# Attention scores of two heads at once in 64-row tiles, in the middle stage of a gated cross-attention block

## The reference, cut to what matters

```python
def _L1_xattn_ref(x, latents, mask, g1, b1, g2, b2, Wq, Wkv, Wout):
    heads, dim_head = (16, 64)
    xn = layer_norm(x, g1, b1)              # x: the context, 16 x 375 x 256
    ln_lat = layer_norm(latents, g2, b2)    # latents: 16 x 112 x 256
    q = ln_lat @ Wq
    kv = jnp.concatenate([xn, ln_lat], axis=1) @ Wkv      # 487 tokens
    k, v = jnp.split(kv, 2, axis=-1)
    ...
    weight = jnp.einsum('bhld,bhnd->bhln', q * scale, k * scale)   # 112 x 487 per head
    weight = jnp.where(full_mask[:, None, None, :], weight, neg)
    weight = jax.nn.softmax(weight.astype(jnp.float32), axis=-1)
    out = jnp.einsum('bhln,bhnd->bhld', weight, v)
    return out.transpose(0, 2, 1, 3).reshape(b, l, heads * dim_head) @ Wout
```

## Time and profile before

| | |
|---|---|
| time, median of 3 runs | 1531.09 us (1529.65 to 1533.0) |
| the profiled execution | 1528.29 us, of which the traced span is 1526.3 us |
| TensorE busy | 1357.1 us, 89% of the span |
| VectorE busy | 1177.2 us, 77% |
| ScalarE busy | 954.2 us, 63% |
| GpSimd busy | 654.9 us, 43% |
| middle stage, first scores to the end of the last batch's slots | 525.0 to 1290.0 us of the span |

### The profile page before, as it was taken

One profiled execution on the slowest core, in us unless ns is written; L12 is line 12 of the kernel. 1 busy time (PEld: TensorE's weight loads), 2 busy tenths in 40 slices (PEclk: granted clock), 3 DMA queues, 4 the chain that ended last, 5 costly groups with the idle time before them and its releaser, 6 DMA issues. The chain is left out here.

```text
span 1526.3 us, 45153 instructions
## 1 busy us (share of the span) xinstructions
PE 1357.1 (89%) x14276; PEld 1053.6 (69%) x14276; DVE 1177.2 (77%) x3350; ACT 954.2 (63%) x2456; POOL 654.9 (43%) x1044
## 2 busy tenths in 40 slices
PE   5999999999974799999999999999999997279995
PEld 3788888888751367776776677767766776278994
DVE  4899999999863388887887877878878787267772
ACT  4887888888951366665666665656656666045663
POOL 3544444444543234342543344334534424235654
PEclk8999999999976899999999999999999999589998
DMA  5333333333201666346653565447634671473323
GB/s 163 100 117 115 115 101 115 115 111 97 72 8 34 130 135 127 88 90 129 144 110 69 120 144 108 91 94 145 125 80 96 130 160 48 136 287 55 61 40 73
DMA packets 167807, 163.36 MB, mean 107 GB/s; under 512 B 81274, under 2 KB 155394, under 8 KB 164528
## 3 DMA queue, kind: packets, MB, share of 16 engines
q1 hardware_dynamic: 151440, 118.80, 34.2%
q0 software_dynamic: 13168, 35.80, 9.3%
q10 hardware_dynamic: 3024, 6.47, 1.5%
HBM read 64.48 MB, written 41.96 MB: 70 GB/s over the span
## 5 line engine op out<-in xcount | busy, mean ns | idle before, releaser
L1414 PE MATMUL b_ps_p<-b_tok_s,w_s 128*128 128x112 f16 (+1 forms) x1536 | 223.3, 300 | 11.3 <-DVE b_k_s L1698 6.6
L1709 DVE CUSTOM_DVE_ANT_0 b_prob<-b_ps_s,b_keep 112x487 f32<-112x487 f32 x256 | 167.9, 656 | 27.4 <-PE b_ps_s L1493 26.3
L1414 PE MATMUL b_ps_p<-w_s,b_tok_s 128*122 128x512 f16 x768 | 186.9, 379 | 0.0
L1605 ACT ACTIVATE b_prob<-b_prob,b_top 112x487 f32<-112x487 f32 x256 | 177.6, 694 | 10.5 <-DVE b_top L1709 10.3
L1414 PEld LDWEIGHTS b_ps_p<-b_tok_s,w_s 128*128 128x128 f16 x1536 | 117.5, 100 | 95.9 <-issue 17.9
L1611 ACT ACTIVATE b_pT<-b_ps_t 122x448 f16<-122x448 f32 x256 | 137.7, 538 | 72.1 <-PE b_ps_t L1501 69.6
L1493 PE MATMUL b_ps_s<-b_k_stack,b_q_dup 128*112 128x487 f16 x512 | 153.4, 382 | 25.6 <-issue 15.9
L1714 DVE TENSOR_TENSOR b_pT<-b_ps_t,b_pT 122x448 f16<-122x448 f32 x256 | 158.6, 619 | 6.9 <-ACT b_pT L1611 5.5
L701 ACT ACTIVATE a_prob<-a_prob,a_top 112x375 f32<-112x375 f32 x256 | 156.4, 611 | 4.4 <-DVE a_top L837 3.4
L837 DVE CUSTOM_DVE_ANT_0 a_prob<-a_ps_s,a_keep 112x375 f32<-112x375 f32 x256 | 138.2, 540 | 24.4 <-PE a_ps_s L593 21.8
L1521 PEld LDWEIGHTS b_ps_o<-b_v_s,b_pT 122*128 122x128 f16 x3072 | 122.5, 98 | 44.3 <-issue 6.6
(11 more groups left out here) (259 smaller groups left out, 3062.1 us busy)
## 6 DMA issues: line engine op xcount, KB each, us to landing
b_k_stack<-b_k_s SPq DMA_DIRECT2D x64, 487.0 KB, 11.0
xs<-a_blank SPq DMA_DIRECT2D x14, 1032.0 KB, 4.0
b_q_dup<-b_q_s SPq DMA_DIRECT2D x128, 112.0 KB, 5.2
c_w_pool<-w_split SPq DMA_DIRECT2D x8, 1600.0 KB, 10.5
b_wch_f<-in_w_experts POOLq DMA_DIRECT2D x32, 384.0 KB, 11.8
w_split<-b_wch_s POOLq DMA_DIRECT2D x32, 384.0 KB, 7.2
a_ctx_f<-in_ctxT SPq DMA_DIRECT2D x16, 375.0 KB, 3.7
a_k_stack<-a_k_s SPq DMA_DIRECT2D x64, 93.8 KB, 2.8
```

What stands on the lines that cost most here:

```text
L1414: last = pe.matmul(out, sta(a, k), mov(m, k), start=(k == 0 and n == 0), stop=(k == tiles - 1 and n == 2))
L1605: act.activation(prob[:, h % RING, 0:NK], prob[:, h % RING, 0:NK], ACT.Exp, bias=top[:, h % RING:h % RING + 1], scale=-1.0, accum_out=sums ...
L1709: dve.tensor_tensor_reduce(prob[:, h % RING, 0:NK], ps_s[h % 2][0:T, 0:NK], keep[par][:, :], -SCALE1, 3e38, ALU.add, ALU.min, top[:, h % R ...
```

## The change

`scores` is called once for two heads, in even slots. It reads the keys and the queries as the products leave them, from `k_s` and `q_s`, which are now double: head `2j` lies in rows 0 to 63 and head `2j+1` in rows 64 to 127. For each of the three `PASSES` it issues two matmuls of 64 rows, one into each score bank, so a pair of heads has six matmuls of 64 rows where it had four of 128 rows. The product of the two low parts is no longer computed. One semaphore increment covers both heads; before a pair TensorE waits for the maxima of both heads before it (`s_max` up to `2 * pair`), where head `h` waited for head `h-2` alone. `k_stack`, `q_dup`, SyncE's `stack` with its 12 transfers for each batch, and the two semaphores go away. The built program gives these matmuls a tile of 64 rows by 128 columns at row 0 or row 64 of the array; every other matmul, before and after, has a tile of 128 rows.

```diff
@@ -1025,10 +1025,8 @@
         keep = [sb(f"keep{i}", [T, NK], F32) for i in range(2)]
 
 
-        q_s = sb("q_s", [128, 2, IT, T], F16)
-        q_dup = [sb(f"q_dup{i}", [128, 2, H, T], F16) for i in range(2)]
-        k_s = sb("k_s", [128, 2, IT, NK], F16)
-        k_stack = [sb(f"k_stack{i}", [128, H, NK], F16) for i in range(2)]
+        q_s = [sb(f"q_s{i}", [128, 2, IT, T], F16) for i in range(2)]
+        k_s = [sb(f"k_s{i}", [128, 2, IT, NK], F16) for i in range(2)]
         v_s = [sb(f"v_s{i}", [128, 2, NB1, INNER], F16) for i in range(2)]
 
 
@@ -1104,8 +1102,6 @@
         s_item = sem("item")
         s_ihi = sem("ihi")
         s_ifree = sem("ifree")
-        s_kstack = sem("kstack")
-        s_qdup = sem("qdup")
         s_score = sem("score")
         s_max = sem("max")
         s_exp = sem("exp")
@@ -1182,22 +1178,6 @@
                 need(sp, s_keep, 1, c, 0, settled)
                 sp.dma_start(keep_u[:, :], mask[c].partition_broadcast(T)).then_inc(s_mload, 16)
 
-            def stack(c, par):
-
-
-                need_all(sp, settled, (s_ihi, PI, c, P_Q), (s_ifree, PI, c, P_Q), (s_score, H, c - 1, 1))
-                for a in range(2):
-                    for part in (HI, LO):
-                        src = k_s[64 * a:64 * a + 64, part, :, :]
-                        rows = part if a == 0 else 1 - part
-                        sp.dma_start(k_stack[par][64 * rows:64 * rows + 64, a::2, :], src).then_inc(s_kstack, 16)
-                need_all(sp, settled, (s_ihi, PI, c, P_V), (s_ifree, PI, c, P_V))
-                for a in range(2):
-                    for rows in range(2):
-                        for part in (HI, LO):
-                            sp.dma_start(q_dup[par][64 * rows:64 * rows + 64, part, a::2, :],
-                                         q_s[64 * a:64 * a + 64, part, :, :]).then_inc(s_qdup, 16)
-
             def residual(c):
                 need(sp, s_hfree, HI_, c, 0, settled)
                 sp.dma_start(x_res[:, :], x2_dram[c]).then_inc(s_rload, 16)
@@ -1211,14 +1191,11 @@
                     residual(b - 1)
                 if ahead(b, 2):
                     load(b + 2)
-                if ahead(b, 1):
-                    stack(b + 1, 1 - par)
                 if not first(b):
                     store(b - 1)
 
             load(0)
             load(1)
-            stack(0, 0)
             run_batches(sp, body)
             residual(B - 1)
             store(B - 1)
@@ -1484,14 +1461,17 @@
                 else:
                     nitem(b + 2, k)
 
-            def scores(b, par, h):
-                if h == 0:
-                    need(pe, s_qdup, 128, b, 128)
-                    need(pe, s_kstack, 64, b, 64)
-                need(pe, s_max, H, b, h - 1)
-                for part in (HI, LO):
-                    last = pe.matmul(ps_s[h % 2][0:T, 0:NK], q_dup[par][:, part, h, :], k_stack[par][:, h, :],
-                                     start=(part == HI), stop=(part == LO))
+            def scores(b, par, pair):
+
+                if pair == 0:
+                    need(pe, s_ihi, PI, b, P_V)
+                    need(pe, s_ifree, PI, b, P_V)
+                need(pe, s_max, H, b, 2 * pair)
+                for n, (a, m) in enumerate(PASSES):
+                    for half in range(2):
+                        rows = slice(64 * half, 64 * half + 64)
+                        last = pe.matmul(ps_s[half][0:T, 0:NK], q_s[par][rows, a, pair, :], k_s[par][rows, m, pair, :],
+                                         start=(n == 0), stop=(n == 2))
                 last.then_inc(s_score, 1)
 
             def transposes(b, h):
@@ -1538,7 +1518,8 @@
 
             def body(b, par):
                 for s in range(H):
-                    scores(b, par, s)
+                    if s % 2 == 0:
+                        scores(b, par, s // 2)
                     if not (first(b) and s < 2):
                         c, _, h = behind(s, 2, b, par)
                         transposes(c, h)
@@ -1579,14 +1560,10 @@
                 ps = ps_p[k % 2]
                 need(act, s_item, PI, c, k + 1)
                 if k < P_Q:
-                    if k == 0:
-                        need(act, s_kstack, 64, c, 0)
-                    act.activation(k_s[:, HI, k, :], ps[:, 0:NK], ACT.Copy).then_inc(s_ihi, 1)
+                    act.activation(k_s[par][:, HI, k, :], ps[:, 0:NK], ACT.Copy).then_inc(s_ihi, 1)
                 elif k < P_V:
                     j = 4 * (k - P_Q)
-                    if j == 0:
-                        need(act, s_qdup, 128, c, 0)
-                    act.activation(q_s[:, HI, j:j + 4, :], ps[:, 0:4 * T].rearrange("p (j n) -> p j n", j=4), ACT.Copy).then_inc(s_ihi, 1)
+                    act.activation(q_s[par][:, HI, j:j + 4, :], ps[:, 0:4 * T].rearrange("p (j n) -> p j n", j=4), ACT.Copy).then_inc(s_ihi, 1)
                 else:
                     j, half = (k - P_V) // 2, (k - P_V) % 2
                     need(act, s_pv, H, c - 1, 0)
@@ -1695,17 +1672,17 @@
                 ps = ps_p[k % 2]
                 need(dve, s_ihi, PI, c, k + 1)
                 if k < P_Q:
-                    dve.tensor_tensor(k_s[:, LO, k, :], ps[:, 0:NK], k_s[:, HI, k, :], ALU.subtract).then_inc(s_ifree, 1)
+                    dve.tensor_tensor(k_s[par][:, LO, k, :], ps[:, 0:NK], k_s[par][:, HI, k, :], ALU.subtract).then_inc(s_ifree, 1)
                 elif k < P_V:
                     j = 4 * (k - P_Q)
-                    dve.tensor_tensor(q_s[:, LO, j:j + 4, :], ps[:, 0:4 * T].rearrange("p (j n) -> p j n", j=4), q_s[:, HI, j:j + 4, :], ALU.subtract).then_inc(s_ifree, 1)
+                    dve.tensor_tensor(q_s[par][:, LO, j:j + 4, :], ps[:, 0:4 * T].rearrange("p (j n) -> p j n", j=4), q_s[par][:, HI, j:j + 4, :], ALU.subtract).then_inc(s_ifree, 1)
                 else:
                     j, half = (k - P_V) // 2, (k - P_V) % 2
                     cols = slice(half * 512, (half + 1) * 512)
                     dve.tensor_tensor(v_s[par][0:KB1, LO, j, cols], ps[0:KB1, :], v_s[par][0:KB1, HI, j, cols], ALU.subtract).then_inc(s_ifree, 1)
 
             def maxima(b, par, h):
-                need_all(dve, settled, (s_score, H, b, h + 1), (s_tr, H, b, h - RING + 1), *([(s_keep, 1, b, 1)] if h == 0 else []))
+                need_all(dve, settled, (s_score, H // 2, b, h // 2 + 1), (s_tr, H, b, h - RING + 1), *([(s_keep, 1, b, 1)] if h == 0 else []))
                 dve.tensor_tensor_reduce(prob[:, h % RING, 0:NK], ps_s[h % 2][0:T, 0:NK], keep[par][:, :], -SCALE1, 3e38,
                                          ALU.add, ALU.min, top[:, h % RING:h % RING + 1]).then_inc(s_max, 1)
 
```

## The result

| | before | after |
|---|---|---|
| median | 1530.37 us (1529.54 to 1533.0) | 1555.68 us (1552.19 to 1557.6) |
| profiled execution | 1528.29 us, span 1526.3 | 1557.32 us, span 1555.4 |

The ratio is 1.0162, 95% interval [1.0144, 1.0179]: the changed kernel is slower by 25 us. Between the two profiled executions lie 29.0 us.

A forecast was written before the change was run, and what follows sets the result against it. TensorE sets the middle stage's pace, VectorE not far behind. Terms of -11, +4.7, +2.5 and +30 sum to +26 us on 1528.29: 1554 profiled, 1557 us median; range 1518 to 1608, the forecast's own 1540 to 1570.

The forecast's parts named there:

- rival B: In each pair, weight loads that aren't hidden lengthen the rounds: +19 us on A, 1546 us; chance 0.10.
- Term 1: At the middle stage's start, the wait for `q_dup`'s transfers and the slow clock behind it go: -11 us.
- term 4: At the pairs of scores, 176 changes between 128-row and 64-row tiles at 0.17 us each: +30 us.
- Terms 2 and 3: Waits for both maxima before pairs: +4.7 us over 15 batches, +2.5 us in the last batch.
- taken up by slot 6: In an odd batch, the delay from slot 0, +0.33 us without changes of tile, is zero at slot 6.
- TensorE starts it at 863.83, the maximum of head 15 ends at 864.30: Slot 0 of an odd batch: the pair waits for that maximum, starts at 864.35, and products come 0.33 us later.
- S: Theory of the experiments: the loss is the changes of tile, the wait is small; 1536 to 1545 us for e1.
- W: Theory of the experiments: most of the loss is the new wait for both maxima; 1556 to 1563 us for e1.
- term 3: In the last batch, pair, maxima and low part form one ring: +0.3 us for each of 8 pairs, +2.5 us.
- A: At the pairs, changes of tile are free and a pass runs side by side: 1527 us; chance 0.25.
- C: In each pair, the six matmuls run one after another: 1609 us, up to 1639 with changes; chance 0.18.
- D: Before the pairs, the waits for maxima don't bind, 0.21 us a pair saved: 1493 us; chance 0.05.

The follow-up runs named there:

- e1: The kernel before, copies kept, with two heads' scores grouped in even slots behind the wait for both maxima, in 128-row matmuls: 1566.72 us.
- e4: The kernel before, with batch 0 alone scored in pairs of 64-row tiles and only its copies left out: 1519.04 us.
- e9: The changed kernel with all six matmuls of a pair on rows 0 to 63, so odd heads get their even neighbours' scores: 1633.54 us.
- e6: The kernel before with one more matmul of 8 columns, 64 rows deep, ahead of each even head's scores: 1565.4 us.
- e7: The kernel before with one more matmul of 8 columns, 128 rows deep, ahead of each even head's scores: 1536.61 us.
- e2: The changed kernel with the pair of scores placed behind the transposes of its slot instead of ahead of them: 1539.63 us.
- e10: e1 with the pair of scores placed behind the transposes of its slot: 1547.7 us.
- e5: The changed kernel with the three matmuls of one half of a pair issued behind one another, then the other half's three: 1556.45 us.

## Why the prediction was right, and where its terms were off

The time, 1557 against 1555.68, came out near the forecast, and the mechanisms that the forecast rests on are there. Two terms were off in opposite directions, though, and that they cancelled is luck. The text's own sign for the pair shows it: it looked for about 1.0 us from the first score to the transposes with changes of tile, 0.8 for rival B, and called itself wrong under 0.75. Measured are 0.75, at that very edge.

**Term 1, -11 us: right.** First scores were forecast at 515.4 and came at 514.40, without a wait for a transfer, and the keys behind them had a granted clock of 1.00. It is 10.4 us by the rows, 11.0 by the medians of e1 and the changed kernel, 11.6 by e4. That the transfers of later batches were worth nothing agrees with e4, which still makes them; no run drops them alone.

**The pair: mechanism right, change of tile over-sized.** The prediction took 0.65 us of rounds and 2 x 0.17 of changes, 0.99. Measured are three rounds of 0.205 (from e9's steps), 0.13 us more up to the transposes, 0.09 ahead and 0.05 in the transposes' own length: 0.62 + 0.27 = 0.89. A change costs 0.095 (e6 less e7, without the turns) to 0.135 us (0.27 / 2), inside the bounds of 0 to 0.19 and not near the upper one. At the prediction's own count of 176 changes term 4 is 17 to 24 us, not 30. Counted over a pair the tiles are then nearly even with what they replace, 0.89 against 0.86, which is why e1 less term 1 gives the changed kernel.

The Trainium skill (TensorEngine Tiling (Array Packing), Tiling Modes, Key Properties) says that a change of mode drains TensorE and that tiles of one mode work independently. The change has a price here, 0.19 us there and back by e6 and e7, though no row shows what happens inside the array; the second holds by e9's 1.37 against 0.76 us. The Trainium skill (TensorE: Matmul & The Clock Gate, Part 3, The mechanism) says in its list of what overlaps that a weight load overlaps a running matmul only where the row groups differ, which was rival B (an earlier sentence of that section also lets a load for the background weight buffer go ahead). In e9 all six loads and matmuls are in one group and a step still takes 0.205 us, no more than the 0.215 of a 128-row score matmul, while each load lasts 0.13 us; the measurement decides, and B falls.

**Terms 2 and 3, the new wait: place right, size too small.** The odd batch can be laid beside the prediction step by step, from starts in the earlier trace rows and the rows above (the end of slot 15 is the turn's start less its idle time, 911.63 and 919.88):

| step | before | after | change | predicted, with changes of tile |
|---|---|---|---|---|
| ranks to slot 0 | 0.05 | 0.99 | +0.94 | +0.52 |
| slot 0 to 10 | 33.76 | 33.82 | +0.06 | +0.89 |
| slot 10 to 12 | 5.23 | 5.97 | +0.74 | +0.45 |
| slot 12 to 14 | 4.93 | 5.34 | +0.41 | +0.41 |
| slot 14 to the end | 3.88 | 3.86 | -0.02 | -0.04 |
| sum | 47.85 | 49.98 | +2.13 | +2.23 |

The predicted column is the text's own: -0.52 taken up by slot 6, -0.2, +0.25 and eight changes of 0.17 give the +0.89; the three steps behind it are -0.21 with 0.49, 0.45 or 0 and one change each. The sum is right, and two of its parts are not.

The waits before slots 12 and 14 were sized well: e1, which has the wait and no 64-row tile, starts its pairs 5.76 and 5.40 us apart, +0.53 and +0.47, where the text had 0.49 and 0.45. What failed is the step "TensorE starts it at 863.83, the maximum of head 15 ends at 864.30". It took that distance from the trace of before. The text's own argument for slots 10 to 14, that TensorE has 0.43 us less to do between a value product and the wait, holds here too, for slot 15 has lost its scores; the maximum of head 15 hangs on the product of slot 14 and comes no earlier. With it the text would have had 0.57 + 0.43 = 1.00 us from the ranks to slot 0; measured are 0.99, and 0.98 in e1. Nor is this taken up by slot 6 in e1: from slot 0 to slot 10 that kernel needs 34.09 us, +0.33, where the text's waits sum to -0.27. In the changed kernel the same stretch is +0.06, although eight changes were charged to it in full. The two differ before slot 2, which e1 reaches 8.03 us behind slot 0 after a wait of 0.55 us for a maximum, the changed kernel 7.61 us behind it after 0.20; why was not separated.

e1 gives the size of the grouping without tiles: 36.1 us. Of its two expectations, that of S, which came from the prediction's terms 2 and 3, was +6 to +15 us; that of W, +25 to +32, had been worked out from the changed kernel's measured loss. Both were too small. The text's own waits are 0.25 + 0.49 + 0.45 = 1.19 us in each of 15 batches, with next to nothing left of the one at slot 0, and 2.5 us in the last: some 20 us, 16 too few. The last batch alone came out at +4.3 us (its ranks' matmul stands 33.5 us behind the one before it, against 29.2) where term 3 had +2.5. On the other side the pair was charged +30 us of changes less some 14 of saved rounds, where the tiles measure about 0 to 4 us (the changed kernel less e1 and e2 less e10, term 1 taken off; 128 x 0.03 = 3.8 by the pair's rows). So the +26 was the sum of a grouping some 16 us too small and of pairs 12 to 16 us too dear.

**The even batch and the turn.** A turn of the loop takes (1132.18 - 713.55) / 4 = 104.66 us, from the first scores behind the first and the last of five turns, against (1115.76 - 716.27) / 4 = 99.87 before; less the odd batch's 2.13 that leaves 2.66 for the even one, where 0.26 + 1.87 = 2.13 were forecast. Of these 2.66 us 0.63 are longer idle time at the turns (3.86 us against 3.23 in the mean of the four), so the batch itself has 2.03. The prediction said that the change does not touch that idle time. It did not hold: the five such waits add up to 15.9 us before and 19.8 after, because three of the five came with two instruction packets close together. This is a property of the built program and not of the tiles: e5, which differs from the changed kernel in the order of six matmuls alone, has no such turn and 16.7 us. Its median is the same all the same, and its profiled execution entered the middle stage 3.0 us later (last value products from 505.77 against 502.76; 505.47 in e4, whose first stage is the same too).

**Rivals.** A falls by e6 less e7, B by e9, C by the pair's 0.75 us and e9's 1.37 without the second row group, D by the 51 waits in the changed kernel. A's time, 1527 us, would by these sizes have been too low even without changes of tile, since the grouping cost some 16 us more than the text had.

## What to carry to other kernels

A wait that is shared by two work items is placed at the earlier item's slot, and what it costs is read from everything queued behind it on that engine: here the grouping cost 36 us, and 19 of them came back when the pair was placed behind work that was ready. Ask where the removed transfers are waited for, and change that place alone: one batch in sixteen held all of the 11 us. When work is taken out of a slot, every wait behind it is reached earlier; each has to be sized with the new arrival, not with the one in the trace. And before two kernels are compared to within a few microseconds, compare their waits at the turns of a hardware loop, which here moved by up to 8 us without being the subject of any edit.

## What the runs showed of the hardware

Two 64-row matmuls in different row groups run side by side even where three of one group stand in a row ahead of the three of the other: 0.76 us for six in e5, as in the alternating order (0.75), where neighbours alone could overlap would have given five steps, 1.0 us. The single records of the pair shown start two by two, at 0, 0.25 and 0.46 us; in e9 they start one by one. If the built program keeps the written order, matmuls of the second group pass those of the first that still wait; the trace doesn't name the half of a record, so this step is inferred. Within one group, weight loads of 64 rows by 112 columns are hidden behind matmuls of 487 columns: in e9 each next load starts with the matmul before it and lasts 0.13 of the 0.205 us of the step. A way from 128-row tiles to 64-row tiles and back costs 0.19 us between short matmuls (e6 and e7). At a turn of the hardware loop TensorE stood 2.8 to 3.7 us, and 4.1 to 4.8 us where two 16-KB instruction packets of queue 8 started within 1.3 us of each other. And with 46.6 MB less traffic, the DMA share in the middle stage down from 0.55 to 0.17, VectorE, ScalarE and GpSimd are busy no less than before (1184.0, 956.4 and 656.4 us against 1177.2, 954.2 and 654.9).
